# Last stage of a mixture-of-experts kernel: every other pair's residual add on GpSimd, half of the loads on ScalarE's queue

## The reference, cut to what matters

```python
h = h + ffn(_layernorm(h))
# in ffn, with K = 2 choices of E = 8 experts for each token:
gates = softmax(top_k(xf @ router_w, 2))
for e in range(E):
    y = layernorm(xf + relu(xf @ w1[e] + b1[e]) @ w2[e] + b2[e]) * gamma[e] + beta[e]
    out = out + w[:, None] * y        # w: the token's gate for expert e, else 0
```

## Time and profile before

| | us |
|---|---|
| median of three executions | 657.08 |
| the three | 649.28, 657.08, 657.23 |
| the profiled execution | 651.72 |
| its span, first to last instruction | 650.2 |
| last scatter lands | 618.14 |
| last sum ends | 646.45 |

### The profile page before, as it was taken

One profiled execution on the slowest core, in us unless ns is written; L12 is line 12 of the kernel. 1 busy time (PEld: TensorE's weight loads), 2 busy tenths in 40 slices (PEclk: granted clock), 3 DMA queues, 4 the chain that ended last, 5 costly groups with the idle time before them and its releaser, 6 DMA issues.

```text
span 650.2 us, 15468 instructions
## 1 busy us (share of the span) xinstructions
PE 486.7 (75%) x4584; PEld 375.8 (58%) x4584; DVE 432.7 (67%) x1725; ACT 326.1 (50%) x734; POOL 354.9 (55%) x499
## 2 busy tenths in 40 slices
PE   1569677987877988787878630799999999998500
PEld 1446355554544655565545420699999999997400
DVE  6866667766555488867645534177777777777657
ACT  2175547655445567665545310355555555555244
POOL 5351123476642375756647674067777777778700
PEclk9698779897877899999878855799999999999955
DMA  4156555345345122223300044778888888878388
GB/s 135 48 146 177 135 145 133 86 109 139 90 137 133 56 68 80 63 64 100 100 26 28 26 160 171 236 231 264 268 273 256 274 271 253 279 251 280 107 326 256
DMA packets 77732, 103.66 MB, mean 159 GB/s; under 512 B 14334, under 2 KB 60705, under 8 KB 77650
## 3 DMA queue, kind: packets, MB, share of 16 engines
q1 hardware_dynamic: 70082, 89.22, 46.2%
q0 software_dynamic: 6416, 12.93, 5.6%
q10 hardware_dynamic: 1152, 0.52, 0.4%
HBM read 74.31 MB, written 34.45 MB: 167 GB/s over the span
## 4 chain that ended last, share of the span: by engine, by line
PE 31%; issue 24%; POOL 11%; SPq 11%; DVE 10%; DMA 8%; ACT 3%; another core or an unknown queue 1%; POOLq 0%; ACTq 0%; DVEq 0%
POOL expert_d L1464 8%; SPq L390 4%; PE avb L767 3%; PE avb L764 3%; DMA stack_d<-kq 3%; PE mbk L722 3%; DMA stk<-stack_d 3%; SPq L407 2%; PE sbk L749 2%; PE sbk L689 2%; PE sbk L896 2%; PE gen L791 2%; POOL sorted_d L1432 2%; PE gen L906 2%; PE mbk L896 2%
## 5 line engine op out<-in xcount | busy, mean ns | idle before, releaser
L1017 DVE TENSOR_REDUCE mx<-mbk 128x4 f32<-128x768 f32 x96 | 91.4, 952 | 64.7 <-PE mbk L722 48.4
L1464 POOL DMA_INDIRECT expert_d<-pexs,dest x103 | 108.5, 1053 | 26.5 <-issue 25.1
L1432 POOL DMA_INDIRECT sorted_d<-pay,slot x96 | 95.6, 996 | 49.5 <-issue 25.0
L548 ACT ACTIVATE pexs<-sbk 128x768 f32<-128x768 f32 x96 | 77.6, 808 | 49.3 <-PE sbk L749 41.1
L616 ACT ACTIVATE pexs<-gen 128x256 f32<-128x256 f32 (+1 forms) x56 | 20.5, 366 | 87.1 <-PE gen L888 81.9
L1459 POOL TENSOR_TENSOR rs<-ve,neghalf 128x2 f32<-128x2 f32 (+1 forms) x56 | 40.6, 725 | 37.4 <-DVE ve L1319 22.3
L722 PE MATMUL mbk<-stk 48*64 48x192 f16 (+1 forms) x512 | 36.5, 272 | 29.0 <-DVE mx L1017 15.5
L749 PE MATMUL sbk<-stk 49*64 49x192 f16 (+1 forms) x512 | 37.0, 270 | 19.1 <-ACT pexs L548 11.5
L1393 POOL TENSOR_TENSOR kept<-h,lnb 128x384 f32<-128x384 f32 x16 | 16.0, 1000 | 62.5 <-DVE h L992 62.5
L722 PEld LDWEIGHTS mbk<-stk 48*64 48x64 f16 (+1 forms) x512 | 13.6, 104 | 51.9 <-issue 38.5
L764 PE MATMUL avb<-pexs,vxs 128*32 128x192 f32 x512 | 40.7, 382 | 2.7 <-issue 2.7
(11 more groups left out here) (221 smaller groups left out, 1232.7 us busy)
## 6 DMA issues: line engine op xcount, KB each, us to landing
stk<-pack_d SPq DMA_DIRECT2D x38, 706.5 KB
pexs<-pack_d SPq DMA_DIRECT2D x18, 706.5 KB
stk<-stack_d SPq DMA_DIRECT2D x64, 144.0 KB
xn<-sorted_d SPq DMA_DIRECT2D x47, 132.0 KB
stack_d<-kq SPq DMA_DIRECT2D x16, 384.0 KB
pack_d<-in_w SPq DMA_DIRECT2D x16, 256.0 KB
stack_d<-kq SPq DMA_DIRECT2D x16, 192.0 KB
sorted_d<-padrow SPq DMA_DIRECT2D x8, 330.0 KB
```

The costliest lines, as they stand in the source:

```text
L548: act.activation(pex[p % 2][m][:, :, :], sbk[:, :, 0:COLS], ACT.Exp, scale=0.25).then_inc(a_pex, 1)
L1017: dve.tensor_reduce(dst, mbk[:, :, 0:COLS].rearrange("p h (c s) -> p h c s", c=2), AX.X, ALU.max).then_inc(d_mx, 1)
L1432: pool.indirect_dma_start(sorted_d[:, :], bass.IndirectOffsetOnAxis(ap=slot[p % 6][:, 2 * k + w:2 * k + w + 1], axis=0), pay[p % 6][:, k, ...
L1464: pool.indirect_dma_start(expert_d[:, :], bass.IndirectOffsetOnAxis(ap=dest[fin % 6][:, k:k + 1], axis=0), ye[fin % 4][:, k, :], None, bou ...
```

## The change

Every odd pair's residual add moves from VectorE to GpSimd, which signals a new semaphore c_psum; the outputs of two pairs wait for one count of c_sum and one of c_psum. The first choices' loads are issued by ScalarE ahead of its multiplies, after the same four waits; SP issues the second choices'. PIECES has (4, 4) in place of (4, 2), (6, 2): six pieces in place of seven.

```diff
-PIECES = ((0, 1), (1, 1), (2, 2), (4, 2), (6, 2), (8, 4), (12, 4))
+PIECES = ((0, 1), (1, 1), (2, 2), (4, 4), (8, 4), (12, 4))
...
+        def all_scattered(eng):
+
+            for i in range(4):
+                last = GRID - 1 - (GRID - 1 - i) % 4
+                eng.wait_ge(ye_out[i], 16 * blocks_to(last, chunks(last) - 1, 4))
+
+        def load_results(eng, i, w):
+
+            q, n = PIECES[i]
+            at = q % GROUP * TILES
+            eng.dma_start((y1, y2)[w][q // GROUP][:, at:at + n * TILES, :], results[w, q // GROUP, :, at:at + n * TILES, :]
+                          ).then_inc(c_in[i], 16)
...
@@ block.sync
-            for i in range(4):
-                last = GRID - 1 - (GRID - 1 - i) % 4
-                sp.wait_ge(ye_out[i], 16 * blocks_to(last, chunks(last) - 1, 4))
...
-            for i, (q, n) in enumerate(PIECES):
-                at = q % GROUP * TILES
-                for w, dst in enumerate((y1, y2)):
-                    sp.dma_start(dst[q // GROUP][:, at:at + n * TILES, :], results[w, q // GROUP, :, at:at + n * TILES, :]
-                                 ).then_inc(c_in[i], 16)
+            all_scattered(sp)
+            for i in range(len(PIECES)):
+                load_results(sp, i, 1)
             for q in range(0, PAIRS, 2):
-                sp.wait_ge(c_sum, q + 2)
+                sp.wait_ge(c_sum, q // 2 + 1)
+                sp.wait_ge(c_psum, q // 2 + 1)
...
@@ block.scalar
+            all_scattered(act)
+            for i in range(len(PIECES)):
+                load_results(act, i, 0)
             for q in range(PAIRS):
                 act.wait_ge(c_in[sum(q >= start for start, n in PIECES) - 1], 32)
...
             for q in range(LATE, PAIRS, 2):
-                act.wait_ge(c_sum, q + 2)
+                act.wait_ge(c_sum, q // 2 + 1)
+                act.wait_ge(c_psum, q // 2 + 1)
...
@@ block.vector
                 ins.then_inc(c_second, 1)
-                dve.wait_ge(c_second, q + 1)
-                dve.tensor_tensor(second_y[:, at:at + TILES, :], second_y[:, at:at + TILES, :], kept[q][:, :, 0:D], ALU.add
-                                  ).then_inc(c_sum, 1)
+                if q % 2 == 0:
+                    dve.wait_ge(c_second, q + 1)
+                    dve.tensor_tensor(second_y[:, at:at + TILES, :], second_y[:, at:at + TILES, :], kept[q][:, :, 0:D], ALU.add
+                                      ).then_inc(c_sum, 1)
...
@@ block.gpsimd
+            for q in range(1, PAIRS, 2):
+                pool.wait_ge(c_second, q + 1)
+                second_y, at = y2[q // GROUP], q % GROUP * TILES
+                pool.tensor_tensor(second_y[:, at:at + TILES, :], second_y[:, at:at + TILES, :], kept[q][:, :, 0:D], ALU.add
+                                   ).then_inc(c_psum, 1)
```

More of the change, by code:

```diff
@@ L339, in early_fusion @@
         b_first, b_dest, b_xb, b_zg, b_y = [sem(n) for n in ("b_first", "b_dest", "b_xb", "b_zg", "b_y")]
-        c_in, c_first, c_second, c_sum, c_out = sems("c_in", len(PIECES)), sem("c_first"), sem("c_second"), sem("c_sum"), sem("c_out")
+        c_in, c_first, c_second, c_sum, c_psum, c_out = sems("c_in", len(PIECES)), sem("c_first"), sem("c_second"), sem("c_sum"), sem("c_psum"), sem("c_out")
         block = ctx.enter_context(nc.Block())
@@ L353, in settled @@
             eng.wait_ge(const_made, 1)
+        results = expert_d.rearrange("(w q p t) d -> w q p t d", w=2, p=P, t=GROUP * TILES)
+        def all_scattered(eng):
[7 more added lines that the diff above has]
+                          ).then_inc(c_in[i], 16)
         @block.sync
@@ L466, in _ @@
                 load_weights(g)
-            for i in range(4):
-                last = GRID - 1 - (GRID - 1 - i) % 4
-                sp.wait_ge(ye_out[i], 16 * blocks_to(last, chunks(last) - 1, 4))
-            results = expert_d.rearrange("(w q p t) d -> w q p t d", w=2, p=P, t=GROUP * TILES)
-            for i, (q, n) in enumerate(PIECES):
-                at = q % GROUP * TILES
-                for w, dst in enumerate((y1, y2)):
-                    sp.dma_start(dst[q // GROUP][:, at:at + n * TILES, :], results[w, q // GROUP, :, at:at + n * TILES, :]
-                                 ).then_inc(c_in[i], 16)
+            all_scattered(sp)
+            for i in range(len(PIECES)):
+                load_results(sp, i, 1)
             for q in range(0, PAIRS, 2):
-                sp.wait_ge(c_sum, q + 2)
+                sp.wait_ge(c_sum, q // 2 + 1)
+                sp.wait_ge(c_psum, q // 2 + 1)
                 o = y2[q // GROUP]
```

## The result

| | before | changed |
|---|---|---|
| executions, us | 649.28, 656.52, 657.08, 657.23 | 664.77, 666.23, 668.03, 671.36 |
| median, us | 656.80 | 667.13 |
| profiled execution, us (span) | 651.72 (650.2) | 671.36 (669.6) |
| last scatter lands | 618.14 | 629.64 |
| last sum ends | 646.45 | 660.39 |

The medians differ by 10.3 us. The median of 667.13 us is above the predicted 656.6 us and outside its range of 649.5 to 661.5.

The account below looks back on a forecast made before the run. The prediction took VectorE's 14 pairs at 1.389 us each to bound the last stage. It summed -0.8 (landing), +2.9 (seven cycles) and +0.05 (signal) to about +2.2 us on 654.40, giving 656.6 us, range 649.5 to 661.5.

Parts of the forecast that it names:

- The step that failed: End of the last stage: after the last add, the last output issues and their landing take 3.75 us, kept unchanged.
- holds nothing back behind it: GpSimd's queue in the last stage: its new wait was said to delay no later work; no cost was added.
- B: Rival, VectorE and GpSimd in the last stage: handover is dear, +5.4 us, 659.8 us; chance 0.07.
- C: Rival, ScalarE's queue in the last stage: six slow load issues delay its multiplies, +7.7 us, 662.1 us; chance 0.05.
- A: Rival, last stage: GpSimd's adds run beside VectorE, cycle 2.30 us; -1.9 us, 652.5 us; chance 0.20.
- Part one, contention: Last-stage adds: each GpSimd add blocks VectorE's two-SBUF-input operations; two-pair cycle 3.20 us instead of 2.78, +2.9 us for seven.
- both overlaps of the earlier trace: Two tiny VectorE operations beside GpSimd adds took 1.64 and 0.89 us (medians 166 and 150 ns), read as standing still.
- Part two, the second queue: Last-stage loads: with half on ScalarE's queue the awaited load lands 0.8 us earlier, bounds 0 and 1.3.
- Part three, the pieces: Loads of pairs 4 to 7 as one piece: landed by 630.5, VectorE needing pair 4 only at 631.2; no cost.
- The sum: Whole last stage: -0.8 for landing, +2.9 for seven cycles, +0.05 for the signal, about +2.2 us.
- the base: Starting time for the whole kernel: the median of the four known executions, 654.40 us, giving 656.6 us.

Follow-up runs that it names:

- the third: Third profile of the unmodified changed kernel, taken on another chip beside the kernel before; 634.37 us against 625.81, ratio 1.0178.
- e1: Kernel before plus one GpSimd memset of 128x1 that waits for the last sum; ratio 1.0094 to the kernel before, +5.9 us.
- e8: Kernel before plus only a GpSimd wait for all the sums; ratio 1.0214 to the kernel before, 1.0144 when repeated on another chip.
- e6: Changed kernel with each GpSimd add replaced by a memset that reads nothing, odd pairs' residual left out; one execution, 634.75 us, no ratio.
- e2: Kernel before with only the odd pairs' adds moved to GpSimd, loads and pieces as before; ratio 1.0111, +6.9 us.
- e4: Changed kernel with the old seven pieces; ratio 1.0117 (1.001 to 1.0224) to the kernel before.
- e7: Kernel before with first choices' loads on ScalarE's queue, old pieces, every add on VectorE; ratio 0.9957, repeated on another chip 1.0013.
- e3: Changed kernel with every add back on VectorE, keeping the split loads and merged piece; ratio 1.0039 to the kernel before, +2.4 us.
- e5: Changed kernel with GpSimd adding only pairs 1, 3, 5 and 7, VectorE all others; ratio 1.0006 to the kernel before.

## Why the prediction was wrong

**The step that failed** is a term of its first paragraph: "Behind the last add come the last two output issues of SP and of ScalarE and their landing: 650.20 - 646.45 = 3.75 us", taken over unchanged into the sum. The change makes GpSimd's end late, and GpSimd's DRAIN ends 9.0 us behind its last instruction. In place of 3.75 us there are 9.2: 5.46 more in the first profile and 5.5 in the third. Where a wait or a small write was the only edit (e1, e8 twice), the tail is 9.4 us, 5.6 to 5.7 more than the 3.7 of before. The row was in the trace of before, 10.75 us long, with its cover: 23.6 us of other work behind its end. The prediction asked what stands behind GpSimd's new wait ("holds nothing back behind it") and counted instructions of the kernel's lines only. None of the rivals had it either: B and C placed their price ahead of the last sum, A in VectorE's cycle and in SP's output issues.

**Part one, contention.** The mechanism was right: one multiply-add beside each GpSimd add is stretched, and e6 shows that it goes when GpSimd doesn't read. The size was off twice. The hold is 0.70 us and not the add's 0.96; 0.18 us of the difference is the multiply-add that was under way when the add started and ran on, and the rest is open. And the odd pair gives back more than the 0.48 of its L1333: its three multiply-adds flow on at 0.79 us in place of 0.91, since the next one starts 0.08 us before the last has ended, where the L1333 behind its wait for c_second started 0.04 us after. The cycle is then 1.38 + 0.79 + 0.70 = 2.87; measured 2.865, forecast 3.20, before 2.77. Over the six cycles up to the last that is +0.6 us; the last, whose GpSimd add nothing overlaps, has +0.4. Together it is the +1.0 of e2, where the forecast had +2.9. The cycle of 2.865 is nearer to the forecast's than to rival A's 2.30, but the hold is not as dear as both overlaps of the earlier trace rows made it look. B is out: no GpSimd add takes more than 0.99 us and no cycle more than 2.87. C is out: ScalarE's six issues cost 0.36 to 0.55 us each, and VectorE's first multiply-add comes at 4.38 in the stage against 4.01.

**Part two, the second queue.** Forecast 0.8 us earlier for pair 2, bounds 0 and 1.3. With one queue it began at 8.47, 8.74 and 8.87 in the kernel before, 8.67 and 8.70 in e2 and e8, and 9.35 and 9.39 in e1 and in e8's repeat. With two it began at 7.83 to 7.96 in e4, e7 and the repeats of the changed kernel, at 8.13 to 8.24 in e3, e5 and e6, and at 9.38 in the first profile. So the gain is some 0.5 to 1.0 us (0.6 for e7 side by side on the third chip), inside the bounds. One landing differs from the next by as much, and in the first pair of profiles pair 2 is 0.5 us later instead.

**Part three, the pieces.** "This costs nothing" was wrong, by 1.2 us at the last sum without GpSimd's adds (e3 against e7; 1.4 at pair 4) and by 0.8 to 0.9 with them (e4 and e2 against the changed kernel). The working set the landing before 630.5 against a pair 4 "only at 631.2"; in the earlier trace rows pair 4 begins at 629.78 (631.16 is pair 5), so there was little cover to begin with, and the landing of the larger piece was not worked out for its new size. In the repeats pair 4 now begins at 11.7, when all four pairs have landed. The gain of part two is so given back.

**The sum.** Forecast +2.2 up to the last sum; measured +2.44 in the first profile and +1.44 in the third. The agreement is chance. In the first profile the parts are +0.5 (landing), +1.0 (adds) and +0.9 (pieces), in the third -0.5, +1.0 and +0.9, against a forecast of -0.8, +2.95 and 0. Behind the last sum the forecast was 0, measured +5.5. A smaller miss is in the base: the step was laid on 654.4 us, the median of four executions with the profiled one among them, and the kernel before measured 656.80.

**What stays open.** The stage explains 6.9 to 7.9 us of a difference that the medians put at 10.3 and the ratio at 12.6 (6.6 to 18.5). Over all comparisons, the difference by ratio stands against that of the traced stage as follows: changed kernel 12.6 against 7.9, 4.3 (2.2 to 6.5) against 6.5 to 6.9, and 11.1 (6.1 to 16.1) against 6.9; e1 5.9 against 6.1; e2 6.9 against 6.4; e8 14.1 (9.8 to 18.4) against 5.6, and 9.0 (5.1 to 12.9) against 6.6. The rest has both signs, so no fixed cost of a late GpSimd end beyond the stage is shown; only e8's first comparison clearly has more than its stage, and its repeat doesn't bear that out. The rest is not outside the traced span: time less span is 1.5 to 1.6 us in all executions of the kernel before and 1.7 to 1.8 in those of the changed kernel, e1 and e8, some 0.2 us more (and 1.9 in e7, where GpSimd's end is early). It is inside the span, then, in executions that no trace shows. Where there are traces, the differences ahead of the stage were in when the scatters begin, and had both signs.

**The better version** is e7: its stage is 30.9 to 31.0 us in both runs, against 31.6 to 32.1 before, but its totals (0.9957 and 1.0013) don't tell it from the kernel before. A version with early GpSimd adds and the old pieces wasn't run; by the measured cycle it would only add contention to e7.

## What to carry to other kernels

Ask for every engine when its program ends, not only its last useful instruction: on GpSimd its end comes 9.0 us after that in every run here, free while others work, and paid but for the 3.7 us of the last outputs where its last add, or even its last wait, moves to the kernel's end. The row of the block end is in the profile of before; the cover behind it belongs in the sum. Before merging loads, set the landing of the merged piece against its first consumer's start, and before giving GpSimd an add beside VectorE's two-input operations, set the hold against the saving: here 0.70 us against 0.60.

## What the runs showed of the hardware that was not expected

- GpSimd's DRAIN at the end of the program: 9.0 us behind its last operation or wait in every run (8979 ns behind a bare wait, 9103 with a memset of 0.10 us in it, 9990 and 10030 with an add of 0.95 or 0.99 us in it). ScalarE's took 396 ns.
- Three multiply-adds of VectorE take 0.91 us of pitch where a wait for its own semaphore and the add follow, and 0.79 where the next multiply-adds follow at once: the wait is the likely reason for the 0.12 us, though the operation behind it differs too.
- A GpSimd add of 0.99 us with all its operands in SBUF stops one of VectorE's two-input operations for 0.70 us; a memset of 1.06 us, none.
- The same kernel took 626 us on some chips and 657 on others; in its three profiles the 103 scatters spread over 190 to 191 us each, and the difference is in where they begin (400.8 against 425.5 and 431.0).
